# Decoder layer on one core: key and query weights centred by matmuls with a constant matrix, the prologue reordered, met waits ahead of TensorE's program

## The reference

```
qkv = einsum('bsh,oh->bso', x, w_qkv)      # 16 query heads, 4 key and 4 value heads of 128
q = layernorm(q, qn_g, qn_b)               # per head: (q - mean(q)) * rsqrt(var + eps) * g + b
k = layernorm(k, kn_g, kn_b)
q, k = rope(q), rope(k)
attn = softmax(q @ k.T / sqrt(128), causal) @ v
x = x + attn @ w_o.T
```

## Time and profile before

| | |
|---|---|
| device time, median of 3 runs | 1494.11 us (1492.78 to 1494.72) |
| the profiled execution's device time | 1493.46 us |
| its span, first to last instruction | 1491.7 us |
| busy: PE, DVE, ACT, POOL | 1373.1, 871.9, 650.3, 393.7 us |
| mean granted TensorE clock | 0.983 |

### The profile page before, as it was taken

How to read it: one execution, slowest core, us unless ns; L and a number is a source line. 1 busy time by engine, 2 the same in 40 slices (tenths; PEclk the granted TensorE clock), 3 DMA queues, 4 the chain that set the end, 5 groups by cost and what they waited for, 6 DMA issues and landing times.

```text
span 1491.7 us, 31431 instructions
## 1 busy us (share of the span) xinstructions
PE 1373.1 (92%) x11264; PEld 875.2 (59%) x11264; DVE 871.9 (58%) x2052; ACT 650.3 (44%) x1447; POOL 393.7 (26%) x311
## 2 busy tenths in 40 slices
PE   2699999999999999979999999999999688999997
PEld 1456666666666666546666666666666444555554
DVE  7876666666666666663444454444444588444433
ACT  2433333333333333444666666666666422322322
POOL 5643333333333333321111111111111084000000
PEclk9799999999999999989999999999999899999999
DMA  8300000000000000201111111121110440000000
GB/s 276 109 1 0 0 0 0 0 0 0 0 0 0 0 0 0 105 20 64 43 60 62 41 41 41 41 62 61 41 41 23 147 164 29 23 1 22 0 23 23
DMA packets 22271, 58.34 MB, mean 39 GB/s; under 512 B 1262, under 2 KB 9454, under 8 KB 19026
## 3 DMA queue, kind: packets, MB, share of 16 engines
q1 hardware_dynamic: 22226, 57.74, 11.7%
HBM read 54.46 MB, written 3.28 MB: 39 GB/s over the span
## 4 chain that ended last, share of the span: by engine, by line
PE 74%; DVE 15%; issue 5%; ACT 2%; POOL 2%; DMA 1%; DVEq 0%; SPq 0%; ACTq 0%; POOLq 0%
PE A L1385 20%; PE A L1353 11%; PE C L1606 10%; PE A L1301 8%; PE C L1409 6%; PE B L1426 5%; PE C L1320 3%; PE A L1621 3%; PE B L1621 3%; DVE ssq L834 2%; PE B L1394 2%; PE B L1312 2%; DVE ub L829 1%; ACT sq L508 1%; DVE ub L830 1%
## 5 line engine op out<-in xcount | busy, mean ns | idle before, releaser
L1301 PE MATMUL A<-arena,xh 128*100 128x512 f16 x768 | 184.1, 383 | 22.6 <-DVE arena L1054 14.3
L1353 PE MATMUL A<-arena,stageb 128*100 128x512 f16 x768 | 176.0, 379 | 28.7 <-DVE stageb L880 28.0
L1385 PE MATMUL A<-wxh,arena 128*122 128x512 f16 x768 | 198.4, 381 | 0.0
L1606 PE MATMUL C<-arena 128*128 128x400 f16 x1024 | 188.4, 338 | 8.7 <-DVE arena L982 8.7
L401 POOL TENSOR_TENSOR region<-tb,ub 100x512 f32<-100x512 f32 x80 | 108.6, 1357 | 294.2 <-DVE ub L830 294.2
L424 POOL TENSOR_TENSOR arena<-arena,region 100x512 f32<-100x512 f32 (+1 forms) x64 | 65.9, 1062 | 427.1 <-DVE region L943 427.1
L1606 PEld LDWEIGHTS C<-arena 128*128 128x128 bf16 x1024 | 101.7, 99 | 85.5 <-issue 15.5
L1301 PEld LDWEIGHTS A<-arena,xh 128*100 128x100 f16 x768 | 94.7, 126 | 93.1 <-issue 20.8
L522 ACT ACTIVATE region<-C,negm 100x100 f32<-100x100 f32 x256 | 84.4, 348 | 147.3 <-DVE negm L869 147.3
L1353 PEld LDWEIGHTS A<-arena,stageb 128*100 128x100 f16 x768 | 92.8, 125 | 94.6 <-issue 34.6
L585 ACT ACTIVATE arena<-C 122x1600 f32<-122x1600 f32 x96 | 144.4, 1504 | 4.6 <-PE C L1409 2.5
(11 more groups left out here) (174 smaller groups left out, 2327.6 us busy)
## 6 DMA issues: line engine op xcount, KB each, us to landing
stageb<-in_wffn SPq DMA_DIRECT2D x16, 768.0 KB, 4.6
arena<-in_ctxt SPq DMA_DIRECT2D x16, 722.0 KB, 4.5
stageb<-in_wffn SPq DMA_DIRECT2D x8, 1024.0 KB, 4.8
arena<-in_wqkv SPq DMA_DIRECT2D x4, 1024.0 KB, 14.0
arena<-in_wffn SPq DMA_DIRECT2D x4, 1024.0 KB, 5.8
out_x<-xres SPq DMA_DIRECT2D x16, 200.0 KB
arena<-in_wx SPq DMA_DIRECT2D x3, 1024.0 KB, 8.5
xres<-in_x SPq DMA_DIRECT2D x1, 3000.0 KB
```

Source lines behind the costliest of these rows:

```text
L1301: ins = pe.matmul(A[j % 2][0:S, :], xp[:, k, :], wp[:, j, k, :], start=(n == 0), stop=(n == 11))
L1353: ins = pe.matmul(A[0][0:S, :], ap[:, h, :], wohl[:, g, part, h % 4, :], start=(n == 0), stop=(n == 47))
L1385: ins = pe.matmul(A[(par + n) % 2][0:rows, :], lhs, wp[:, 0 if n == 0 else 1 if n < 4 else 2, k, :], start=(i == 0), stop=(i == 11))
L1606: ins = pe.matmul(C[2 * (e % 2) + half][:, 0:UB * S], wf[:, 3 * (e // 4) + half, k, (e % 4) * 128:(e % 4 + 1) * 128], part[:, k, :], start ...
```

## The change

**Centring.** The constants get a 128 x 128 matrix `C_CEN`, the identity less 1/128. The host lays pieces 0 to 4 out with a head's 128 outputs on the partitions. PE's new `centre(j)` makes 16 products of f32, 128 x 128 each, of the raw weight and that matrix, which come out centred and in the old layout in the four banks `C`; it is done in two halves of two banks. ACT's `w_centred` (two of 128 x 1024 a piece) writes the high half from PSUM, DVE's `w_centred_lo` the remainder. A half of `centre(j)` waits for DVE to have read the same banks of piece j - 1 (`d_cen`). `w_mean`, `wmean`, POOL's subtractions and `idh` go.

**Order.** PE centres piece j + 1 before it projects piece j. DVE makes `x_lo(0)` ahead of the rope tables, `w_lo(5)` after `proj(0, 2)`, batch 1's row statistics ahead of `proj(0, 4)`, and puts `w_lo(6)` and `w_lo(7)` between the `z_back`s. ACT makes `w_hi(5)` after the third square and `w_hi(6)` to `w_hi(9)` after `x_hi(1)`. SP issues `x` of batch 0 first, then the constants, piece 0, gains and biases, the other pieces, `x` of batches 1 and 2 after piece 5, pieces 6 to 9 (8 and 9 once their place has been centred from), and `x` of batches 3 to 15 last.

**Waits.** Before PE's first transpose stand `FILL` = 320 waits for a semaphore value that `credit` has already set. In the built program they are 158 instructions of two waits, and the rest is joined to the three that wait for constants, `xn` and `a_v`. In the loops PE's waits that another one implies go: in `project`, `project_out`, `project2`, `scores2` and before some transposes. That is 5 instructions of the attention loop's turn and 17 of a double turn of the cross-attention; with the ends, about 207 in an execution. The head of the cross-attention loop lies 2,051 PE instructions into the program, before 1,586, if a matmul is counted with its weight load and an f32 product as two of each; the loop's body has 1,659 of them, before 1,676.

```diff
+FILL = 320
...
+    c[:, C_CEN:C_CEN + D] = np.eye(D) - 1.0 / D
...
@@ sync
-            sp.dma_start(cst[:], consts).then_inc(ld_c, 16)
-            sp.dma_start(gain[:], gains).then_inc(ld_c, 16)
-            sp.dma_start(bcol[:], bcols).then_inc(ld_c, 16)
             xt = x.rearrange("(b p) f -> p b f", b=NB)
             sp.dma_start(xres[:, 0, :], xt[:, 0, :]).then_inc(ld_x0, 16)
+            sp.dma_start(cst[:], consts).then_inc(ld_c, 16)
             for j in range(10):
                 if j >= 8:
 
-                    sp.wait_ge(a_whi, j - 7)
-                    sp.wait_ge(d_wlo, j - 7)
+                    sp.wait_ge(pe_cen, 2 * (j - 7))
                 dst, loaded, _ = staged(j)
                 sp.dma_start(dst, wqkv[:, j] if j < 6 else wo[:, j - 6]).then_inc(loaded, 16)
+                if j == 0:
+                    sp.dma_start(gain[:], gains).then_inc(ld_g, 16)
+                    sp.dma_start(bcol[:], bcols).then_inc(ld_g, 16)
                 if j == 5:
-                    sp.dma_start(xres[:, 1:NB, :], xt[:, 1:NB, :]).then_inc(ld_x, 16)
+                    sp.dma_start(xres[:, 1:3, :], xt[:, 1:3, :]).then_inc(ld_x1, 16)
+            sp.dma_start(xres[:, 3:NB, :], xt[:, 3:NB, :]).then_inc(ld_x, 16)
@@ scalar
+            def w_centred(j, half):
+
+                act.wait_ge(pe_cen, 2 * j + half + 1)
+                act.activation(wqh[:, j, 2 * half:2 * half + 2],
+                               Call[:, half * 1024:half * 1024 + 1024].rearrange("p (k n) -> p k n", k=2),
+                               ACT.Copy, scale=SW).then_inc(a_cen, 1)
...
             x_hi(0)
-            for j in range(3):
-                w_hi(j)
+            for half in range(2):
+                w_centred(0, half)
             for j in range(5):
+                if j < 4:
+                    for half in range(2):
+                        w_centred(j + 1, half)
                 square(0, j)
-                w_hi(j + 3)
+                if j == 2:
+                    w_hi(5)
             v_of(0)
             x_hi(1)
-            for j in range(8, 10):
+            for j in range(6, 10):
                 w_hi(j)
@@ vector
+            def w_centred_lo(j, half):
+
+                dve.wait_ge(a_cen, 2 * j + half + 1)
+                dve.scalar_tensor_tensor(wql[:, j, 2 * half:2 * half + 2].rearrange("p k n -> p (k n)"),
+                                         Call[:, half * 1024:half * 1024 + 1024], SW,
+                                         wqh[:, j, 2 * half:2 * half + 2].rearrange("p k n -> p (k n)"),
+                                         ALU.mult, ALU.subtract).then_inc(d_cen, 1)
...
+            for half in range(2):
+                w_centred_lo(0, half)
+            for j in range(5):
+                if j < 4:
+                    for half in range(2):
+                        w_centred_lo(j + 1, half)
+                proj(0, j)
+                if j == 2:
+                    w_lo(5)
+                elif j == 3:
+                    dve.wait_ge(ld_x1, 16)
+                    row_stats(1, ssq[:, 20:21])
             head_norm(0)
             normed(1, rstd[:, 20:21])
+            z_back(0, 0)
+            x_lo(1)
+            z_back(0, 1)
             w_lo(6)
-            x_lo(1)
+            z_back(0, 2)
+            z_back(0, 3)
             w_lo(7)
-            for g in range(5):
-                z_back(0, g)
+            z_back(0, 4)
@@ tensor
+            def centre(j):
+
+                src, loaded, n = staged(j)
+                pe.wait_ge(loaded, n)
+                for half in range(2):
+                    if j > 0:
+                        pe.wait_ge(d_cen, 2 * (j - 1) + half + 1)
+                    for k in (2 * half, 2 * half + 1):
+                        for h in range(4):
+                            ins = pe.matmul(C[k][:, h * D:(h + 1) * D], src[:, h, k * 128:(k + 1) * 128],
+                                            cst[:, C_CEN:C_CEN + D], start=True, stop=True)
+                    ins.then_inc(pe_cen, 1)
...
             def scores2(b, u):
-                t = (2 * u + 1) // NC
-                wait(pe, "a_T", b, t + 1)
-                wait(pe, "d_T", b, t + 1)
+                if u == 0:
+                    wait(pe, "a_T", b, 1)
+                    wait(pe, "d_T", b, 1)
...
-            pe.wait_ge(ld_c, 48)
-            pe.wait_ge(g_setup, 1)
+            for _ in range(FILL):
+                wait(pe, "pe_xT", -1, 1)
+            pe.wait_ge(ld_c, 16)
             x_turn(0)
-            for j in range(6):
-                pe.wait_ge(a_whi, j + 1)
-                pe.wait_ge(d_wlo, j + 1)
+            centre(0)
+            for j in range(5):
+                if j < 4:
+                    centre(j + 1)
+                pe.wait_ge(d_cen, 2 * j + 2)
                 project(0, j)
+            pe.wait_ge(d_wlo, 1)
+            project(0, 5)
```

More of the change, by code:

```diff
@@ L202, in build @@
         fsc = sb("fsc", [128, 16])
-        idh = sb("idh", [128, 128], F16)
         statc = sb("statc", [S, 6])
@@ L240, in build @@
         ld_c = sem("ld_c")
+        ld_g = sem("ld_g")
+        ld_x1 = sem("ld_x1")
         ld_x0 = sem("ld_x0")
@@ L384, in _ @@
             credit(pool, "g")
[L385 to L392, removed]
             def w_of(b, j):
@@ L451, in ones @@
                     .then_inc(g_ones, 1)
-            pool.wait_ge(a_whi, 13)
-            pool.wait_ge(d_wlo, 13)
+            pool.wait_ge(a_whi, 8)
+            pool.wait_ge(d_wlo, 8)
             ones(0)
@@ L481, in _ @@
             credit(act, "a")
+            def w_centred(j, half):
[3 more added lines that the diff above has]
+                               ACT.Copy, scale=SW).then_inc(a_cen, 1)
             def w_hi(j):
                 src, loaded, n = staged(j)
-                if j < 5:
-                    act.wait_ge(g_wcen, j + 1)
-                else:
-                    act.wait_ge(loaded, n)
-                if 6 <= j < 10:
-                    act.wait_ge(d_wlo, j - 3)
+                act.wait_ge(loaded, n)
+                if 6 <= j < 9:
+                    act.wait_ge(pe_cen, 2 * (j - 3))
+                if j == 9:
+                    act.wait_ge(d_wlo, 1)
                 dst = wqh[:, j] if j < 6 else wohl[:, j - 6, 0] if j < 10 else wxh[:, j - 10]
@@ L1029, in _ @@
             normed(0, rs1[:, 0:1])
-            dve.wait_ge(ld_c, 48)
+            x_lo(0)
+            dve.wait_ge(ld_c, 16)
+            dve.wait_ge(ld_g, 32)
             for w, g in ((0, 2), (1, 0)):
@@ L1057, in w_lo @@
                    .then_inc(d_wlo, 1)
-            w_mean(0)
-            x_lo(0)
-            w_mean(1)
-            for j in range(2, 5):
-                w_mean(j)
-                w_lo(j - 2)
-            proj(0, 0)
-            for j in range(3, 6):
-                w_lo(j)
-                proj(0, j - 2)
-            proj(0, 4)
-            dve.wait_ge(ld_x, 16)
-            row_stats(1, ssq[:, 20:21])
+            for half in range(2):
[10 more added lines that the diff above has]
+                    row_stats(1, ssq[:, 20:21])
             head_norm(0)
             normed(1, rstd[:, 20:21])
+            z_back(0, 0)
+            x_lo(1)
+            z_back(0, 1)
             w_lo(6)
-            x_lo(1)
+            z_back(0, 2)
+            z_back(0, 3)
             w_lo(7)
-            for g in range(5):
-                z_back(0, g)
+            z_back(0, 4)
             def turn(b, first=False, last=False):
@@ L1113, in _ @@
             turn(0, first=True)
+            dve.wait_ge(ld_x, 16)
             with dve.Fori(0, NB - 3) as i:
@@ L1290, in project @@
                 if j == 0:
-                    wait(pe, "a_xhi", b, 1)
                     wait(pe, "d_xlo", b, 1)
@@ L1294, in project @@
                 elif j >= 2:
-                    wait(pe, "a_sq", b, j - 1)
-                    wait(pe, "d_t", b, j - 1)
                     wait(pe, "d_u", b, j - 1)
@@ L1365, in project2 @@
                 if n == 0:
-                    wait(pe, "a_x2", b, 1)
                     wait(pe, "d_x2", b, 1)
@@ L1369, in project2 @@
                 elif n == 1:
-                    wait(pe, "a_ctx", b, 1)
                     wait(pe, "d_ctx", b, 1)
@@ L1567, in turn @@
                 if end < 1:
-                    wait(pe, "a_x2", b + 2, 1)
                     wait(pe, "d_x2", b + 2, 1)
@@ L1581, in turn @@
                 if end < 2:
-                    wait(pe, "a_T", b + 1, 1)
-                    wait(pe, "d_T", b + 1, 1)
                     turn_heads(b + 1, 1, odd)
@@ L1669 @@
     q, k, v = wqkv[:H * D], wqkv[H * D:(H + HKV) * D], wqkv[(H + HKV) * D:]
-    wqkv = tiles(np.concatenate([k, q, v]))
-    wqkv = wqkv.reshape(128, KT, 6, 512).transpose(0, 2, 1, 3)
+    heads = np.concatenate([k, q]).reshape(5, 4, D, DM).transpose(2, 0, 1, 3)
+    wqkv = np.concatenate([heads, tiles(v)[:, None]], 1)
     wo = tiles(f["L0_attn_w_o"]).reshape(128, 4, 4, DM)
```

20 lines of the change are left out of this document (5 added, 15 removed).

## The result

| | before | after |
|---|---|---|
| median of 20 runs each, us | 1493.52 (1490.43 to 1495.84) | 1496.36 (1493.56 to 1499.98) |
| ratio | | 1.0019, 95% interval 1.001 to 1.0028 |
| span of the profiled execution, us | 1491.7 | 1491.7 |
| its mean granted clock | 0.983 | 0.986 |

A forecast was written before the change was run, and what follows sets the result against it. PE was taken as the bound, busy 1373.1 of 1491.7 us, with the change acting in the prologue. `head_norm` 4.2 later less 1.4 given back left 2.8 on 1493.46: 1496.3, put as 1496; range 1485 to 1502.

The forecast's parts named there:

- The fill: Head of PE's program: 161 instructions of met waits at 0.11 us, 17.7 us, putting the first transpose at 21.1.
- B: Rival at PE's head: waits cost only 0.051 us each, PE at the transposes at 11.6, total 1486.5; chance 0.18.
- `xn`: Prologue, batch 0: with `x` loaded first, `xn` is ready near 9.5 us, before PE reaches its first transpose.
- A: The forecast case for the whole kernel: 1496 us, own range 1492 to 1500; chance 0.58.
- C: Rival at PE's head: waits cost 0.156 us each, PE at 28.5, 7.4 us later, total 1503.5; chance 0.08.
- The pace: Prologue centring and projecting: PE sets the cycle at 3.6 + 2.6 = 6.2 us a weight; projection 3 ends at 52.8.
- `head_norm`: Prologue, behind DVE's last rope part: takes 2.6 us, its end moving from 57.5 to 61.8, taken as 4.2 later.
- The first transposes: Prologue, behind `head_norm`: PE's transposes of POOL's products begin at +1.3 us instead of +3.7.
- The give-back: Behind `head_norm`: DVE's new order ends the row maxima at +16.1 us instead of +17.5, returning 1.4.
- The waits taken out: PE's loops: about 207 implied waits removed bring 0 us; 23 us if none were hidden.
- Rival D: Cross-attention loop over one program stretch too many: 6 jumps wait, 2 us each gives 1508, at most 1524; chance 0.09.

The follow-up runs named there:

- five waits a place: The fastest kernel with 5 instead of 3 met waits before each matmul of the first centrings and projections (but each group's first): 1523.57 us, ratio 1.0215.
- no waits: The change without its 320 met waits at the head of PE's program (FILL = 0): 1490.92 us, ratio 0.9987.
- the fastest kernel: The spread waits alone, plus `w_hi(5)` and `w_lo(5)` one projection earlier: 1482.06 us, ratio 0.9934; measured again 1483.14, ratio 0.9931.
- the spread waits alone: The change with its head waits replaced by three met waits before each matmul, except each group's first, of the centrings and first projections: 1485.28 us, ratio 0.996.

## Why the prediction was right

The forecast was 1496, against 1496.36, by its own likeliest case, and its path through the prologue held. That it came within 0.4 us is luck: single runs of the change lie 6 us apart, and two terms behind the first projections were off by 0.85 and 0.65 us in opposite directions. Step by step:

- **The fill.** PE at the first transpose at 21.1, measured 20.77; the price of 0.11 for an instruction of met waits, measured 0.107 and 0.111. That the recorded length of 0.051 is not the price was the decision that mattered (B rested on it). The Trainium skill (Perfetto Trace Analysis, Sequencer-only Instruction) says that the record shows the execution of such an instruction alone, without what comes before and behind it; the rows agree, 0.051 recorded and 0.11 from one to the next.
- **`xn`** was taken as ready at 9.5 and was at 7.71. This changed nothing: PE comes later than both in A, in C and in B (11.6). Only without the fill does it set the start (7.73).
- **The pace.** 6.2 us a weight, set by PE: measured 6.16. The ends of projections 0 and 3 were forecast at 34.1 and 52.8 and came at 33.6 and 52.1, projection 4 at 54.0 to 56.6 and came at 53.86 to 56.66.
- **`head_norm`** was mis-sized: +4.2 forecast, +5.05 measured. The last rope part ended where it should (59.36 for 59.2), but the chain behind it took 3.3 us where 2.6 was taken from the earlier trace rows: its first operation, of 100x20 elements, took 0.81 us, before 0.17. The row of 0.17 was the exception already in the kernel before, as the view of this line over its 16 executions shows (count, ns min/median/max, first and last start):

```profile
L840 DVE TENSOR_SCALAR ssq<-ssq x16: 167/818/821, 55.0 to 612.3; 100x20 f32<-100x20 f32 x16
```

In the other 15 of before, and in all 16 of the change, a POOL product on 100x512 is running when it starts, and it ends 0.03 to 0.04 us after that product (in the prologue of the change 60.17 against 60.14). In the one of 0.17 the row statistics stand in between and POOL is idle. The change took them out of there, so this operation of the prologue came to lie beside the product, and the price was to be had from the loop's turns. In all twelve traces 190 executions start beside a product and take 0.8, and the two that don't take 0.17; no run was made that takes only the product away.
- **The first transposes** behind `head_norm` were forecast at +1.3 and came at +2.1, since `xn` of batch 1, for which PE transposes first, took 1.36 us and not 0.55. Such is its time in the attention loop too, where POOL's product starts 0.04 behind it. Yet before, in the prologue, it took 0.55 with the same start of the product, and the product took 3.60:

```profile
57.53 0.55 DVE L803 TENSOR_SCALAR xn<-xres,mv,rstd 100x512 f32<-100x512 f32 x1
57.57 3.60 POOL L409 TENSOR_TENSOR region<-region,rstd 100x512 f32<-100x512 f32 x1 [2.84 <-DVE rstd L787]
```

Which of the two engines gives way differs, then, and what decides it stays open.
- **The give-back** was mis-sized the other way: +16.1 forecast for the end of the row maxima behind `head_norm`, +15.4 measured, so 2.05 came back and not 1.4. The two errors left 3.0 for 2.8. The trace shows POOL's products unhindered, as was forecast (5.21 for 9.64), but the reason given fails: with the old order they take 5.21 as well, because `w_lo(6)` comes only when ACT has made `w_hi(6)`, behind `x_hi(1)`. What the new order avoids in the new kernel is DVE's wait for ACT with the `z_back`s behind it, 4.6 us, which was not seen.
- **The waits taken out** at nothing: confirmed alone.
- **Rival D** was rightly named and placed, and does not occur at this place of the loop. Its price was too low: a missed jump was put at 0 to 4.6 us and costs 7.1, because the clock falls behind the hole. The Trainium skill (Runtime: NRT & Kernel Launch, Instruction fetch mechanics) says that a jump out of the window waits for a load; the traces agree, with holes of 4.1 to 4.95 us. The reading of its 128 KB as eight usable blocks does not hold: a body over eight stretches missed, over seven never. Nor does its window of two pages, which the prediction left out: by it every jump back over this body would wait, and over seven stretches none did (0.53 us).

The change without its fill's cost is a gain, which the prediction did not separate: with the waits where they cost nothing, the same edit gives 0.4% (0.25 to 0.56) and with one step of DVE moved 0.7%. The fill, 320 waits at an idle head, brings the loop to a place where it fits and gives away 9 us by the ratios (11.7 at the loop's start) for it.

## What to carry to other kernels

Waits that are met were free between matmuls of 0.23 us up to two instructions of 0.11, and paid one by one where the engine stood idle: a program that must be padded is padded in its busy part. A loop whose body is nearly as long as what PE holds of its program should be tried at several places, and read from three things: holes marked "issue" behind the jump, the packet count of the instruction queue, and the spread of the runs. An edit of the prologue moves every loop behind it, and 136 instructions that cost the prologue 0.5 us made the whole kernel 2.7% slower (1483.14 to 1523.57). A duration that is read off one row should be looked up in the line's other executions: here the one of the prologue was 0.17 us and the other fifteen 0.82.

## What was not expected of the hardware

- A hole of PE costs more than its length: after each of the six missed jumps TensorE ran wholly or partly at the lower level for some 5 us, which cost 2.6 us a jump beside the hole's 4.5.
- The loop over eight stretches missed all six jumps at one place (five waits a place, 84 packets) and two of six at another (no waits, 47 packets), whose runs spread over 30 us, about four misses of 7.1. By the estimated edges, some 5 instructions of the body lie behind the last edge in the second, and some 21 in the first. That the number of misses changes there from run to run is read from the spread of the times, since one execution alone was traced, and why it does stays open.
- Kernels with the same code behind the attention loop differ by 2 us in the feed-forward (303.1 to 305.3) and by 4 in the cross-attention (544.97 to 548.8), in the cross-attention by stretches at a lower granted clock that come in one execution and not in the next: 0.91 for some 40 us from 651 in the second measurement of the fastest kernel, 1.00 there in the first; and once behind a hole of 1.67 us (the spread waits alone). With this, effects under 2 us can't be told from the time, only from the timeline.
